# Image rows mirrored and folded around a column transform, with fp32 matmuls in halves of the array

## The reference, cut to what matters

```python
# x: (8, 56, 56, 256) float32
x = x + conv(gn(x));  t = to_tokens(x)
t = t + attention(ln(t));  t = t + ffn(ln(t))

def conv(x):                                  # D1 = 512 channels
    xn = simple_rms(x)
    u = silu(xn @ W_u.T + b_u)
    v = silu(xn @ W_v.T + b_v)                # (8, 56, 56, 512)
    g = rpe_coeffs(...)                       # (111, 111, 512): one coefficient for each offset
    vf = rfft2(v, s=(112, 112)); af = rfft2(wrapped(g))
    y = irfft2(vf * af)[:56, :56]             # a 2-D convolution, channel by channel
    return (u * y) @ W_o.T + b_o + x
```

## Time and profile before

| | us |
|---|---|
| median of 3 runs | 5406.36 (5403.94 to 5410.94) |
| the profiled execution: span | 5398.1 |
| of it `kr`, to 664 | 664 |
| `pr`, 664 to 1279 | 615 |
| gap, 1279 to 1299 | 20 |
| `co`, 1299 to 2847 | 1548 |
| `mx`, 2847 to 3918 | 1071 |
| `at` and `ff` | 1480 |

### The profile page before, as it was taken

How to read it: one execution, slowest core, us unless ns; L and a number is a source line. 1 busy time by engine, 2 the same in 40 slices (tenths; PEclk the granted TensorE clock), 3 DMA queues, 4 the chain that set the end, 5 groups by cost and what they waited for, 6 DMA issues and landing times. The chain is left out here.

```text
span 5398.1 us, 89326 instructions
## 1 busy us (share of the span) xinstructions
PE 5214.1 (97%) x27048; PEld 3662.3 (68%) x27048; DVE 3997.7 (74%) x6176; ACT 2512.3 (47%) x4791; POOL 2489.9 (46%) x1381
## 2 busy tenths in 40 slices
PE   8999899997999999999998999999989999987999
PEld 6777655554555555555556777777767777765999
DVE  6777666666999999999996676766635666665887
ACT  5555577774434334343434555555532222211555
POOL 0000054443999999999995555555301111111332
PEclk9999999998999999999999999999999999998999
DMA  3222167775444444444446666666533333433443
GB/s 109 89 89 72 53 197 219 217 217 170 149 150 150 149 152 148 152 148 150 151 136 182 195 203 200 191 200 202 163 113 97 104 113 107 118 89 97 123 122 113
DMA packets 349121, 782.62 MB, mean 145 GB/s; under 512 B 43433, under 2 KB 147845, under 8 KB 339460
## 3 DMA queue, kind: packets, MB, share of 16 engines
q1 hardware_dynamic: 326596, 703.91, 44.2%
q10 hardware_dynamic: 22400, 77.08, 4.0%
HBM read 420.49 MB, written 360.38 MB: 145 GB/s over the span
## 5 line engine op out<-in xcount | busy, mean ns | idle before, releaser
L928 POOL TENSOR_TENSOR co_prod<-co_cross 111x512 f32<-111x512 f32 x448 | 848.8, 1895 | 0.0
L862 ACT ACTIVATE co_y_out<-co_y_ps 112x512 f32<-112x512 f32 x448 | 267.9, 598 | 928.2 <-PE co_y_ps L808 923.1
L925 POOL TENSOR_TENSOR co_prod<-co_direct 111x512 f32<-111x512 f32 x448 | 576.3, 1286 | 203.8 <-PE co_y_ps L808 116.0
L902 DVE TENSOR_TENSOR co_direct<-co_v_ps,co_spec 111x1024 f32<-111x1024 f32 x448 | 543.5, 1213 | 92.0 <-PE co_v_ps L135 87.9
L2012 POOL TENSOR_TENSOR at_t<-at_t,at_p_bias 112x1024 f32<-112x1024 f32 x56 | 137.7, 2470 | 889.3 <-DMA at_t<-t_tiles 889.3
L904 DVE TENSOR_TENSOR co_cross<-co_v_ps,co_spec 111x1024 f32<-111x1024 f32 x448 | 541.5, 1209 | 0.0
L135 PE MATMUL co_v_ps<-co_v_high,co_col_fwd_high 112*111 112x512 f32 x896 | 506.1, 565 | 1.4 <-DVE co_cross L904 1.4
L806 PE MATMUL co_y_ps<-co_prod,co_col_inv 111*112 111x512 f32 x896 | 458.2, 592 | 0.0
L808 PE MATMUL co_y_ps<-co_prod,co_col_inv 111*112 111x512 f32 x896 | 457.5, 592 | 0.1
L882 DVE TENSOR_TENSOR co_v_low<-co_v_in,co_v_high 112x1024 fp32r<-112x1024 f32 x224 | 372.3, 1662 | 0.0
L135 PE MATMUL co_v_ps<-co_v_low,co_col_fwd_high 112*111 112x512 f32 x896 | 354.3, 395 | 0.0
(11 more groups left out here) (277 smaller groups left out, 14268.5 us busy)
## 6 DMA issues: line engine op xcount, KB each, us to landing
v_rows<-pr_rows_out SPq DMA_DIRECT2D x56, 1792.0 KB, 8.2
co_v_in<-v_rows SPq DMA_DIRECT2D x448, 224.0 KB
y_rows<-co_y_out SPq DMA_DIRECT2D x448, 224.0 KB
mx_y_in<-y_rows SPq DMA_DIRECT2D x224, 448.0 KB, 5.5
kr_x_in<-x SPq DMA_DIRECT2D x56, 448.0 KB, 3.9
kern_rows<-kr_rows_out SPq DMA_DIRECT2D x28, 896.0 KB, 4.7
pr_x_in<-x SPq DMA_DIRECT2D x112, 224.0 KB
mx_x_in<-x SPq DMA_DIRECT2D x56, 448.0 KB, 5.3
```

Source lines behind the costliest of these rows:

```text
L862: nc.scalar.activation(y_out[:, b, :], y_ps[b % 2][:2 * SIDE, :], ACT.Copy).then_inc(y_ready, 1)
L902: nc.vector.tensor_tensor(direct[b % 2][:], v_ps[b % 2][:POINTS, :], spec[i][:, :2 * WIDE], ALU.mult).then_inc(real_terms, 1)
L925: nc.gpsimd.tensor_tensor(prod[b % 2][:, :WIDE], direct[b % 2][:, :WIDE], direct[b % 2][:, WIDE:], ALU.subtract).then_inc(real_ready, 1)
L928: nc.gpsimd.tensor_tensor(prod[b % 2][:, WIDE:], cross[b % 2][:, :WIDE], cross[b % 2][:, WIDE:], ALU.add).then_inc(combined, 1)
```

## The change

The 56 image rows are put in another order on the host, so that a chunk holds four rows and the four that mirror them. In `pr` the two tiles of a pair are added (GpSimd, `add_rows`) and subtracted (VectorE, `subtract_rows`) before the row transform; in `mx` the sum and the difference of what comes back are formed again (`take_odd` on ScalarE, `unfold` on VectorE), and the product with the gate moves to GpSimd (`mix`). In `co` the folded column has real matrices of 56 rows: `forward` and `inverse` are two fp32 matmuls each, in halves of the array, nothing is split, VectorE makes one instruction of 111x2048 and GpSimd one of 111x1024 for an image. The output's rows are put back on the host. SP's transfers are the same in number and size; the input of an image pair is loaded into a buffer that is free once `forward` has read it.

```diff
 columns_phase
-        col_fwd = [T.sb(f"col_fwd_{part}", [2 * SIDE, 2, POINTS], F32R) for part in parts]
+        col_fwd = T.sb("col_fwd", [128, POINTS])
+        terms = [T.sb(f"terms{i}", [POINTS, TERMS * WIDE]) for i in range(4)]
+        prod = [T.sb(f"prod{i}", [POINTS, 2 * WIDE]) for i in range(4)]
-        LAG = 2
+        LAG = 3
+        RING = len(prod)
+                def spectrum(k, out, part):
+                    if out == 0 and part == 0:
+                        pe.wait_ge(taps_loaded, k * 32 + 32)
+                        pe.wait_ge(spec_ready, k)
+                    matrix = ((0, 1), (2, 0))[out][part]
+                    last = nc.tensor.matmul(taps_ps[:POINTS, bass.ts(out, WIDE)], col_taps[:, matrix, :], taps_in[:, part, :],
+                                            start=part == 0, stop=part == 1)
...
                 def forward(k, b):
-                        last = product(nc, v_ps[b % 2][:POINTS, bass.ts(out, WIDE)], [w[:, out, :] for w in col_fwd],
-                                       [x[:, b, :] for x in v], start=True, stop=True)
+                    for part in range(2):
+                        side = slice(part * GAP, part * GAP + SIDE)
+                        last = nc.tensor.matmul(v_ps[b % 2][:POINTS, bass.ts(part, WIDE)], col_fwd[side, :], v_in[side, b, :],
+                                                start=True, stop=True)
                 def inverse(k, b):
+                        for part in range(2):
+                            last = nc.tensor.matmul(y_ps[b % 2][part * GAP:part * GAP + SIDE, :],
+                                                    col_inv[:, part * SIDE:(part + 1) * SIDE],
+                                                    prod[b % RING][:, bass.ts(part, WIDE)], start=True, stop=True)
                 def step(k, i, more, more2):
                     for b in range(LAG, BATCH):
-                        if b == BATCH // 2 + 1 and more:
-                            spectrum(k + 1)
+                        if more and b > LAG:
+                            spectrum(k + 1, *divmod(b - LAG - 1, 2))
                         forward(k, b)
                         inverse(k, b - LAG)
 scalar
                 def step(k, i, more, more2):
                     for b in range(BATCH):
-                        if b == BATCH // 2 and more:
-                            spectrum(k + 1, 1 - i)
-                        if ahead:
-                            split_v(*ahead)
+                        if more and b >= TERMS:
+                            spectrum(k + 1, 1 - i, b - TERMS)
+                        wait_inverse(act, k, b)
...
+                        nc.scalar.activation(y_out[:, b, :], y_ps[b % 2][:SPAN, :], ACT.Copy).then_inc(y_ready, 1)
 vector
                     dve.wait_ge(spec_ready, k + 1)
+                        nc.vector.tensor_tensor(terms[b % RING][:].rearrange("p (t n) -> p t n", t=2),
+                                                v_ps[b % 2][:POINTS, :].unsqueeze(1).to_broadcast(twice),
+                                                spec[i][:].rearrange("p (t n) -> p t n", t=2), ALU.mult).then_inc(multiplied, 1)
 project_phase, gpsimd
-                for n in range(1, GROUPS * GROUP):
-                    normalise(n // GROUP, n % GROUP)
+                for n in range(last + 1):
+                    add_rows(n // GROUP, n % GROUP, 1)
+                    if n + GROUP <= last:
+                        normalise((n + GROUP) // GROUP, n % GROUP)
+                    if n < last:
+                        add_rows((n + 1) // GROUP, (n + 1) % GROUP, 0)
 mix_phase, gpsimd
+                for g in range(2 * PAIRS):
+                    mix(g, 0)
+                    mix(g, 1)
+                    if g + 2 < 2 * PAIRS:
+                        normalise((g + 2) // 2, g % 2)
+                    mix(g, 2)
+                    mix(g, 3)
+                    if g + 1 < 2 * PAIRS:
+                        residual((g + 1) // 2, (g + 1) % 2, first=g == 0)
```

More of the change, by code:

```diff
@@ L60, in angles, with mirrored_rows, folded_slots @@
     return 2.0 * np.pi * ((np.outer(a, b) % POINTS) / POINTS)
+HALF_ROWS = CHUNK_ROWS // 2
+def mirrored_rows():
+    order = []
+    for first in range(0, SIDE // 2, 2):
+        order += [first, first + 1, SIDE - 1 - first, SIDE - 2 - first]
+    return np.array(order)
+def folded_slots():
+    place = np.arange(SIDE)
+    return place // CHUNK_ROWS * HALF_ROWS + place % HALF_ROWS, place % CHUNK_ROWS >= HALF_ROWS
 def shape_constants():
@@ L821, in step @@
                         inverse(k, BATCH - LAG + b)
-                pe.sem_inc(inv_mm, SLOTS)
-                spectrum(0)
+                pe.sem_inc(inv_mm, BATCH)
+                pe.wait_ge(consts_in, 16 * len(loads))
+                for piece in range(4):
+                    spectrum(0, *divmod(piece, 2))
+                pe.wait_ge(y_clear, SLOTS)
                 for b in range(LAG):
@@ L868, in _ @@
-                split_taps(0)
-                for pair in range(HIGH_AHEAD):
-                    split_v(0, pair)
-                spectrum(0, 0)
+                for col in range(TERMS):
+                    spectrum(0, 0, col)
                 with act.Fori(0, LOOP) as s:
@@ L952, in project_phase @@
         v = [T.sb(f"v{t}", [SPAN, WIDE]) for t in range(TILES)]
+        fold = [T.sb(f"fold{t}", [SPAN, WIDE]) for t in range(TILES)]
         rows_out = [T.sb(f"rows_out{u}", [ROWS, CHUNK_ROWS, WIDE]) for u in range(2)]
@@ L1083, in row_pass @@
                         side = slice(r * GAP, r * GAP + SIDE)
-                        last = nc.tensor.matmul(row_ps[t % 2][r][:ROWS, :], row_fwd[side, :], v[t][side, :], start=True, stop=True)
+                        last = nc.tensor.matmul(row_ps[t % 2][r][:ROWS, :], row_fwd[side, t % 2, :], fold[t][side, :],
+                                                start=True, stop=True)
                     last.then_inc(row_mm, 1)
@@ L1519, in step @@
                     if now:
+                        inverse_rows(*now, 0)
+                        inverse_rows(*now, 1)
                         gate_mm(*now, 2)
                     if before:
+                        turn_gated(*before, 3)
                         output_mm(*before, 2)
-                        turn_gated(*before, 3)
                     if after:
@@ L1539, in step @@
                     if now:
-                        if after:
-                            gate_mm(*after, 0)
+                        turn_gated(*now, 1)
                         output_mm(*now, 0)
-                        turn_gated(*now, 1)
+                    if after:
+                        gate_mm(*after, 0)
                     if before3:
@@ L1547, in step @@
                     if now:
-                        inverse_rows(*now, 2)
-                        inverse_rows(*now, 3)
-                        if after:
-                            gate_mm(*after, 1)
+                        turn_gated(*now, 2)
                         output_mm(*now, 1)
-                        turn_gated(*now, 2)
+                    if after:
+                        gate_mm(*after, 1)
                     if later:
@@ L1776, in step @@
                     if now:
-                        low_part_mixed(*now, 0)
-                        mix(*now, 1)
+                        unfold(*now, 1)
+                        low_part_mixed(*now, 1)
+                    if before:
+                        residual(*before, 1)
                     if before2:
@@ L1782, in step @@
                         scale_gate(*after, 0)
[L1783 to L1784 removed]
                     if now:
[L1786 to L1787 removed]
+                        low_part_mixed(*now, 2)
                     if before3:
                         take_norm(*before3)
[L1790 to L1791 removed]
                     if before:
```

361 lines of the change are left out of this document (177 added, 184 removed).

## The result

The changed kernel takes 5665.53 us (median of 4 runs, 5640.88 to 5678.19), the kernel before 5405.15 beside it (5401.48 to 5410.94). The ratio is 1.047, with a 95% interval of 1.045 to 1.050. The profiled execution has a span of 5676.4 us, 278 more than before. The forecast was 5345, and the range ended at 5445.

What follows compares the result with a forecast made beforehand. TensorE, busy 96 to 100% of all three stages, was taken to bound the kernel. The profiled 5398.1 us - 139 (column) + 85 (projection) + 0 (mix) gave 5344, with 8 around it 5352, shaded to 5345; range 5190 to 5445.

Steps and rivals of the forecast that it cites:

- TensorE's items in the column stage: Column stage: each pair of half matmuls or spectrum matmul takes 0.86 plus 0.18 us for changing tiling, 1.04.
- rival 1: Column stage: tiling changes cost little between halves, `co` takes 1200 to 1300 us, the kernel 5150 to 5240; chance 0.13.
- The added wait: Column stage: the spectrum's fourth copy, behind image 6's result, stops TensorE about 3.7 us a round; rounds of 24.6 us.
- The clock: Column stage: the new pause lowers TensorE's clock in one round of three, 1.7 us each, 32 us in all.
- Rival 3: Column stage: TensorE falls to 1.2 GHz every round, 1.9 us each, 106 us; kernel 5426; chance 0.13.
- The projection stage: GpSimd's fold stands behind normalising, which waits for a load, so `row_pass` is late: 85 us more, range 30 to 130.
- if one step is late by w, the next is late by 3.1 - w: Projection stage: the fold's lateness from step to step, settling at 1.5 us on the mean, 52 x 1.5 = 78.
- The mix stage: Added copies, sums and moved products fit; a chunk stays at 18.5 us: 0 change, range -5 to +60.
- Rival 4: Mix stage: products queue behind GpSimd's waits, each chunk late by 1 to 2 us; kernel 5400 to 5457; chance 0.11.
- my sum of -54: Whole kernel: column stage 139 us less, projection stage 85 more, mix stage 0.
- Rival 1's lower sum: Whole kernel: the low end of cheap tiling changes, 5406 - 350 + 85, given as 5150 us.

Runs made afterwards that it cites:

- e10: Changed kernel with the edits of e5, e3, e7 and e8, and TensorE's four spectrum matmuls in a row; 5035.67 us, 0.932 of the kernel before.
- e5: Changed kernel with e1's edit and two buffers for the rows the spectrum is made from; 5293.48 us, 0.979 of the kernel before.
- e1: Changed kernel with ScalarE's four spectrum copies made together ahead of image 4's result; 5784.89 us, 1.071 of the kernel before.
- e3: Changed kernel with GpSimd's fold ahead of normalising, which waits for a load, in the projection stage; 5525.06 us, 1.022 of the kernel before.
- e7: Changed kernel with ScalarE's copy of the second pair's odd rows ahead of the fourth gate; 5581.53 us, 1.031 of the kernel before.
- e8: Changed kernel with VectorE's inversion and shift ahead of unfolding the second pair; 5589.05 us, 1.035 of the kernel before.
- e6: Changed kernel with e2's spread of the spectrum's copies and e5's two buffers; 5460.71 us, 1.010 of the kernel before.
- e2: Changed kernel with spectrum copies moved half way: two ahead of image 4's result, one of image 5's, one of image 6's; 5764.72 us, 1.066 of the kernel before.

## Where the prediction held and where it failed

- **TensorE's items in the column stage**: 1.04 us forecast, 1.03 measured; VectorE's product 2.29 us for 2.2, GpSimd's sum 2.36 for 2.4. Right, and rival 1 fell: e10 shows that the change of tiling is what costs.
- **The added wait**: 3.79 us for 3.7, at the place and for the reason given. Right. e5 shows that it was worth more than its length: without it and the clock's falls a round is 6.6 us shorter.
- **The clock**: the step that failed first. I took a fall in one round of three, 3.4 us long, at 1.7 us. It falls in every round, for 6.8 us, of which TensorE works 6.24; a round of 24.6 became 27.2, 2.6 us. 56 x 2.6 = 146 us stand where I put 32, and the granted clock in `co` is 0.88 where I wanted it above 0.9. Rival 3 named this mechanism and priced it at 1.9 us; it had 13 in 100, though the row behind it showed one pause of this length and one fall behind it. Nothing in the rows spoke for one in three.
- **The load of the spectrum's rows** wasn't in the working at all. It was hidden in the changed kernel, and it decides what removing the pause is worth (e1 against e5).
- **The projection stage**: 85 forecast, 170 measured. The place (the fold behind a wait for a load) is right, e3. My own recurrence, "if one step is late by w, the next is late by 3.1 - w", held for the first eight chunks: the waits swing about 1.5 and neighbours add up to 3.0 or so (1.65 and 1.40, 1.84 and 1.13). The step that failed is that nothing in the sum let the clock fall in this stage. Behind the first fall the recurrence no longer holds (4.2 and 0.7): the waits came to 113 us for my 85, and the work at 1.2 GHz cost 53 that I had put at nothing.
- **The mix stage**: 0 forecast, 115 measured. I followed TensorE's and GpSimd's lists, and the way from `inverse_rows` to `turn_gated`, but not the order on ScalarE and VectorE, where the new copy stands behind a gate that waits and loads a table. Rival 4 had the size, 1 to 2 us a chunk, but by GpSimd's queue; e7 and e8 show that it was the copy of odd rows and the shift.
- **The balance**: 18 gained, 170 and some 115 lost, and 10 at the ends are the 278 us of span. Each of the three misses alone would have turned the sign of my sum of -54: it becomes +67, +31 or +61. Rival 1's lower sum was off by a little (5406 - 350 + 85 is 5141, not 5150); nothing hung on it.

The Trainium skill (TensorE: Matmul & The Clock Gate, HAM oscillation) tells of a loop that falls to the lower clock in each pass from the pauses between its bursts. The trace agrees: 56 falls in 56 rounds of the column stage, and about one in two chunks of the projection stage from 778 us on. e5 and e3 show that it ends with the pauses.

## What to carry to other kernels

Where a change adds a pause of TensorE to a loop that had none, price it by its length and by a fall of the clock behind each, and look for what pauses in the other stages too. Of every instruction that a change puts into an in-order queue, ask what the instruction ahead of it waits for; the largest losses here were two or three lines of order, and each came back with the order turned. Before a wait is removed, look for the load that it hides: here one edit alone cost 2%, and with its buffer it brought 6.6%.

## What the runs showed that I had not expected

- A pause of 1.64 us, once in 24 us, was followed by 3.4 us at 1.2 GHz in nearly every round (e6); one of 3.8 us by 6.8, and one of some 6.5 us (e1) by 6.8 or 10.2. In e2 the same short pause had a fall behind it in only 18 of 54 rounds. Pauses of 1.3 us in 20.6 in the mix stage brought none. What decides between these cases is open.
- In the projection stage waits of about 1.5 us a chunk went on for eight chunks without a fall, then the falls came and kept coming: behind each fall stands a longer wait, and at the longer wait the next fall. e3 shows that the falls end with the waits; that a fall in its turn lengthens the next wait is my reading, and what starts the first fall was not tried. Its moment differs from trace to trace, and the changed kernel's time varies by 37 us where the kernel before varies by 9.
- TensorE can be kept without any gap for 1100 us, with halves of the array in turn, beside VectorE at 87%, GpSimd at 91% and DMAs at 0.67.
